# A scan and a feed-forward part joined into one program: quantisation beside the last scan group, last projection inside the first feed-forward step

## The reference

```python
# layer 0, first half
x_in = inp - mean(inp)
x, z = split(x_in @ W_in)                    # 256 + 256
x = silu(depthwise_conv4(x) + conv_b)
Bm, Cm = split(x @ W_x)                      # 16 + 16 states
delta = softplus(x @ W_dt + b_dt)
h[t] = exp(delta[t] * A) * h[t-1] + delta[t] * B[t] * x[t]   # for each of 256 x 16
y[t] = sum_s h[t, s] * C[t, s]
out = ((y + x * D) * silu(z)) @ W_out + inp
x = layernorm(x + out)
# layer 0, second half
xq, wq = fp4_quant_dequant(x), fp4_quant_dequant(w)   # blocks of 16: scale = max|.|/6, round to a grid
h = silu(xq @ wq_gate.T) * (xq @ wq_up.T)    # 352 hidden
x = layernorm(x + fp4_quant_dequant(h) @ wq_down.T)
# layer 1: attention, layernorm, three dense layers of signs, layernorm
```

## Time and profile before

| | |
|---|---|
| timed runs | 1086.28, 1090.7, 1086.28 us, median 1086.28 |
| the profiled execution | time 1083.86 us, span 1082.1 us |
| TensorE busy | 923.6 us (85%), 4482 matmuls; mean granted clock 0.959 |
| VectorE busy | 919.0 us (85%) |
| ScalarE busy | 726.4 us (67%) |
| GpSimd busy | 791.7 us (73%) |
| costliest groups | GpSimd drives 128 x 2359 ns; accumulations 512 x 622 ns; scans 184 x 1218 ns (into PSUM) and 72 x 1203 ns (into SBUF) |
| first VectorE instruction | 5.49 us |
| last scan product of VectorE | 470.83 us |
| first instruction of the third block | 483.54 us |
| first gate product | 488.02 us |

### The profile page before, as it was taken

How to read it: one execution, slowest core, us unless ns; L and a number is a source line. 1 busy time by engine, 2 the same in 40 slices (tenths; PEclk the granted TensorE clock), 3 DMA queues, 4 the chain that set the end, 5 groups by cost and what they waited for, 6 DMA issues and landing times. The chain is left out here.

```text
span 1082.1 us, 15503 instructions
## 1 busy us (share of the span) xinstructions
PE 923.6 (85%) x4482; PEld 482.3 (45%) x4482; DVE 919.0 (85%) x1446; ACT 726.4 (67%) x1536; POOL 791.7 (73%) x576
## 2 busy tenths in 40 slices
PE   6697989898979797756986779999999997799995
PEld 2233434343434342333654555555555543345454
DVE  4799999999999999967885477898989985689996
ACT  4776868686868686534565457777777767777872
POOL 2899999999998989945777734666676634877672
PEclk9899999998999999988899899999999999999998
DMA  4752515252535353006000222333333220000001
GB/s 149 311 235 78 236 78 229 85 211 102 197 116 197 117 197 117 1 23 122 1 0 11 87 80 85 95 90 90 91 87 97 84 60 3 1 1 11 19 20 30
DMA packets 35164, 103.97 MB, mean 96 GB/s; under 512 B 3659, under 2 KB 22475, under 8 KB 24395
## 3 DMA queue, kind: packets, MB, share of 16 engines
q1 hardware_dynamic: 35095, 103.16, 27.9%
HBM read 93.84 MB, written 8.91 MB: 95 GB/s over the span
## 5 line engine op out<-in xcount | busy, mean ns | idle before, releaser
L586 PE MATMUL m_yac<-m_hC,ident 128*128 128x512 f32 x512 | 255.7, 622 | 60.7 <-POOL m_hC L554 22.1
L544 POOL TENSOR_TENSOR m_dBu<-m_du,m_Bt 128x1024 f32<-128x1024 f32 x128 | 299.6, 2359 | 10.7 <-DMA m_Bt<-bcd 9.7
L331 DVE TENSOR_TENSOR_SCAN m_dA<-m_dA,m_dBu 128x512 f32<-128x512 f32 x184 | 222.2, 1218 | 17.1 <-ACT m_dA L456 13.3
L1302 DVE TENSOR_REDUCE a_nm<-bank 128x2 f32<-128x512 f32 x256 | 168.9, 683 | 43.0 <-PE bank L1533 41.0
L1472 ACT ACTIVATE late<-bank 128x512 f32<-128x512 f32 x256 | 150.5, 598 | 72.0 <-PE bank L1533 70.4
L586 PEld LDWEIGHTS m_yac<-m_hC,ident 128*128 128x128 f32 x512 | 93.3, 195 | 205.3 <-issue 111.3
L456 ACT ACTIVATE m_dA<-m_delta,early 128x510 f32<-128x510 f32 x256 | 169.9, 677 | 0.3
L340 DVE TENSOR_TENSOR m_hC<-m_dA,m_Ct 128x512 f32<-128x512 f32 x184 | 122.7, 667 | 0.0
L554 POOL TENSOR_TENSOR m_hC<-m_hS,m_Ct 128x512 f32<-128x512 f32 x72 | 94.7, 1315 | 24.8 <-DVE m_hS L331 24.8
L1533 PE MATMUL bank<-ks,qs 72*128 72x256 bf16 x512 | 98.8, 276 | 15.9 <-DMA ks<-parts 8.0
L453 ACT ACTIVATE m_dA<-m_zero 128x2 f32<-128x2 f32 x181 | 31.3, 173 | 114.0 <-DVE m_hC L340 113.5
(11 more groups left out here) (218 smaller groups left out, 1851.4 us busy)
## 6 DMA issues: line engine op xcount, KB each, us to landing
m_Bt<-bcd SPq DMA_DIRECT2D x32, 1024.0 KB, 6.1
m_Ct<-bcd SPq DMA_DIRECT2D x32, 1024.0 KB, 6.6
qs<-parts SPq DMA_DIRECT2D x16, 576.0 KB
ks<-parts SPq DMA_DIRECT2D x48, 192.0 KB
parts<-a_part SPq DMA_DIRECT2D x32, 192.0 KB, 2.2
out<-x_all SPq DMA_DIRECT2D x8, 256.0 KB, 2.3
vx<-in_vrow SPq DMA_DIRECT2D x4, 256.0 KB
qs<-in_fill SPq DMA_DIRECT2D x1, 768.0 KB
```

Of the source, the lines that this page charges most:

```text
L331: nc.vector.tensor_tensor_scan(out, decay, dBu[:, g % RD], 0.0, ALU.mult, ALU.add).then_inc(scan_ready, 1)
L544: nc.gpsimd.tensor_tensor(dBu[:, g % RD:g % RD + CH], du[:, n % 2], Bt[:, s].unsqueeze(1).broadcast_to([P, CH, GTOK]), ALU.mult).then_inc( ...
L586: return nc.tensor.matmul(out, lhsT, rhs, start=start, stop=stop)
L1302: nc.vector.tensor_reduce(nm[:, slot % 2, q, 2 * pair:2 * pair + 2], s1[i % 2][:], AX.X, ALU.max, negate=True).then_inc(max_ready, 1)
```

## The change

There is one block. SyncE's loads stand at the head of its part of it (`load`). The scan's functions now take a second argument `beside(i)`, called after each unit i of the last group, and return a `tail(n)`, which is interleaved piece by piece with the feed-forward steps n = -1, 0 and 1.

- `beside`: VectorE quantises x group 0 at units 4 (scales), 6 (abs, magic) and 15 (back), GpSimd its middle at 10; TensorE turns the weights at 1, 6 and 11 and x group 0 at 18, ScalarE copies at 8, 13, 18 and 25. They share bank 4. The scales of x group 0 lie in PSUM bank 5, not in SBUF, so the projection of group 6 (unit 16) waits for `qx.back`.
- `tail`: VectorE's `leave` of the last group in step -1, piece 2; `project_out` in step 0, piece 5, `squares` piece 6, `rstds` piece 7; `normalize` in step 1, piece 1.
- The product back of x group 1 is issued in step 0, piece 1, not at the end of step -1.
- PSUM: the scan uses banks named for the whole kernel, decays in 7, 0, 2, 1, sums in 6 and 3, the rest in 4 and 5. SBUF: the scan's tiles are given back and later parts' tiles lie over them; the turned weights lie where the weights were.
- SyncE's loads of constants wait for the last `normalize`.

The diff, cut to its core (indentation as after; the bodies of the scan's functions are the same):

```diff
-    with ctx:
...
-        dA = [ps(f"dA{i}", [P, 2, SEQ]) for i in range(RA)]
-        yac = [ps(f"yac{c}", [P, GTOK]) for c in range(CH)]
-        pp = [ps(f"pp{i}", [P, GTOK]) for i in range(2)]
+    ctx.close()
+    dA = [k.bank[i][:].rearrange("p (a b) -> p a b", a=2) for i in (7, 0, 2, 1)]
+    yac = [k.bank[i] for i in (6, 3)]
+    pp = k.bank[4:6]
...
+    def vector(dve, beside):
-            for n in range(GROUPS + 1):
+        for n in range(GROUPS):
...
-                        if n == GROUPS:
-                            quant_scale(nc, dve, k, k.qx, ffn_blocks(k, 0), 0)
-                            quant_abs(nc, dve, k.qx, 0)
-                            quant_magic(nc, dve, k.qx, 0)
...
+                if n + 1 == GROUPS:
+                    beside(i)
...
-            dve.wait_ge(norm_chain, GROUPS)
+        def tail(n):
+            for u in range(m.MARKS):
+                if n == -1 and u == 2:
+                    leave(GROUPS - 1)
+                yield
...
+                if n == 0 and u == 6:
+                    squares(GROUPS - 1)
+                if n == 1 and u == 1:
+                    normalize(GROUPS - 1)
...
+                if n == 0 and u == 7:
+                    rstds(GROUPS - 1)
...
+            if m == GROUPS - 2:
+                pe.wait_ge(k.qx.back, 1)
...
+                if n == 0 and u == 5:
+                    project_out(GROUPS - 1)
...
+    wts = k.wts[:]
+    wgT = wts[:, 0:HID]
...
+    def beside_vector(dve):
+        def at(i):
+            if i == 4:
+                dve.wait_ge(scan.z_took, 2 * GROUPS)
+                dve.wait_ge(scan.norm_chain, 1)
+                quant_scale(nc, dve, k, qx, ffn_blocks(k, 0), 0)
+            if i == 6:
+                quant_abs(nc, dve, qx, 0)
+                quant_magic(nc, dve, qx, 0)
+            if i == 15:
+                quant_back(nc, dve, qx, 0)
...
-        back_x(0)
...
+            if n == 0:
+                back_x(1)
...
-            if has(n + 2):
+            if has(n + 2) and n >= 0:
                 back_x(n + 2)
...
+    def beside_gpsimd(pool):
+        def at(i):
+            if i == 10:
+                quant_middle(nc, pool, qx, 0)
...
+    def beside_scalar(act):
+        def at(i):
+            if i in (8, 13):
+                n = (i - 8) // 5
+                act.wait_ge(w_turned, n + 1)
+                nc.scalar.activation((wgT, wuT)[n], th[0][:, 0:HID], ACT.Copy).then_inc(w_copied, 1)
...
+            if i == 25:
+                took_x(act, 0)
...
+    def beside_tensor(pe):
...
+            if i == 18:
+                pe.wait_ge(w_copied, 3)
+                turned_x(pe, 0)
...
+                if n == 0 and j == 1:
+                    pe.wait_ge(scan.y_step, 2 * GROUPS)
...
     def sync(sp):
+        sp.wait_ge(scan.norm_chain, GROUPS)
         sp.dma_start(k.identb[:], k.identb_dram).then_inc(k.identb_loaded, 16)
...
+            scan_end = scan_part(eng, beside_part(eng))
             ffn = ffn_part(eng)
-            for n in range(-1, f.LONE):
+            for n in range(-1, 2):
+                side_by_side(ffn(n), f.MARKS, scan_end(n), m.MARKS)
+            for n in range(2, f.LONE):
                 alone(ffn(n))
```

More of the change, by code:

```diff
@@ L703, in ffn_phase, with sb, sem, col @@
-def ffn_phase(nc, k):
+    def sb(name, shape, dt=F32):
+        return ctx.enter_context(nc.sbuf_tensor("m_" + name, shape, dt))
+    def sem(name):
+        return k.ctx.enter_context(nc.semaphore("m_" + name))
+    def col(name):
+        a, b = MAMBA_COLS[name]
+        return k.mprm[:, a:b]
+    w_in, w_x, w_dt, w_out = col("w_in"), col("w_x"), col("w_dt"), col("w_out")
+    conv_r, conv_b, b_dt, skip, decay = (col(x) for x in ("conv_r", "conv_b", "b_dt", "skip", "decay"))
+    ident = k.ident[:]
@@ L1010, in step, with turned_x @@
             yield
-            m = n + 1
-            if has(m):
-                act.wait_ge(x_turned, m + 1)
-                wait(act, up_ready, GT * (m - 1))
-                nc.scalar.activation(xqT[:, m % 2], th[0][:], ACT.Copy).then_inc(x_copied, 1)
+            if has(n + 1) and n >= 0:
+                took_x(act, n + 1)
             yield
         return step
+    def turned_x(pe, m):
+        pe.wait_ge(x_back, m + 1)
+        wait(pe, h_copied, min(GT * (m - 3) + 3, GT * GROUPS))
+        src = qx.out.rearrange("p (a b) e -> p a (b e)", a=GT)
+        for j in range(GT):
+            last = nc.tensor.transpose(th[0][:, P * j:P * j + P], src[:, j], k.ident[:])
+        last.then_inc(x_turned, 1)
@@ new lines, in beside_tensor, with at @@
+    def beside_tensor(pe):
+        ident = k.ident[:]
+        wq = qw.out.rearrange("p b e -> p (b e)")
+        def at(i):
+            if i == 1:
+                pe.wait_ge(qw.back, 1)
+                pe.wait_ge(scan.z_took, 2 * GROUPS - 1)
+            if i in (1, 6):
+                n = (i - 1) // 5
+                wait(pe, w_copied, n)
+                for c, (at, rows) in enumerate(HC):
+                    a = (len(HC) * n + c) * DM
+                    last = nc.tensor.transpose(th[0][:, at:at + rows], wq[0:rows, a:a + DM], ident[0:rows, 0:rows])
+                last.then_inc(w_turned, 1)
+            if i == 11:
+                pe.wait_ge(w_copied, 2)
+                for c, (at, rows) in enumerate(HC):
+                    a = 2 * len(HC) * DM + at
+                    last = nc.tensor.matmul(th[0][0:rows, P * c:P * c + P], wq[:, a:a + rows], k.center[:],
+                                            start=True, stop=True)
+                last.then_inc(w_turned, 1)
+            if i == 18:
+                pe.wait_ge(w_copied, 3)
+                turned_x(pe, 0)
+        return at
@@ L1020, in tensor @@
     def tensor(pe):
         ident = k.ident[:]
-        pe.wait_ge(qw.back, 1)
-        wq = qw.out.rearrange("p b e -> p (b e)")
-        for n, dst in enumerate((gp[0], up[0])):
-            for c, (at, rows) in enumerate(HC):
-                a = (len(HC) * n + c) * DM
-                last = nc.tensor.transpose(dst[:, at:at + rows], wq[0:rows, a:a + DM], ident[0:rows, 0:rows])
-            last.then_inc(w_turned, 1)
-        for c, (at, rows) in enumerate(HC):
-            a = 2 * len(HC) * DM + at
-            last = nc.tensor.matmul(th[1][0:rows, P * c:P * c + P], wq[:, a:a + rows], k.center[:],
-                                    start=True, stop=True)
@@ L1101, in step @@
             yield
-            turn_x(n + 1)
+            if has(n + 1) and n >= 0:
+                turned_x(pe, n + 1)
             down(n - 2, 3)
```

968 lines of the change are left out of this document (488 added, 480 removed).

## The result

| | before | after |
|---|---|---|
| median of the timed executions, us | 1088.49 (4: 1086.28 to 1092.75) | 1075.51 (4: 1073.02 to 1080.87) |
| profiled execution, time and span, us | 1083.86, 1082.1 | 1077.57, 1075.8 |
| its mean granted TensorE clock | 0.959 | 0.957 |

The ratio is 0.9899, with a 95% interval of 0.9868 to 0.9929: 11.0 us faster, between 7.7 and 14.4 (the two medians themselves lie 13.0 apart). The forecast was 1076.5 us and 9.8 us faster.

The account below looks back on a forecast made before the run. VectorE was taken to bound the last scan group, and chains of short links the start and seam. Gains of 1.3 and 8.5 (12.5 + 1.0 - 5.0) sum to 9.8 us: 1086.28 to 1076.5, range 1071 to 1082.

Parts of the forecast that it names:

- The start, +1.3: Kernel start: without waiting for the load block, the first convolution matmul comes at about 9.8 instead of 11.05, gaining 1.3 us.
- This time does not move: Start: the w_out product's weight load, released by the DMA of the parameters' last part, still begins at 8.41 us.
- The term's lower end, 0: Start: gain 0 if TensorE is at its lower clock level in the convolution's first matmuls.
- The last group, +5.0: Last scan group: VectorE pays 5.0 us net for eight added operations of the first x group (3.85 - 0.71 + 1.9).
- The wait of abs: Last scan group: abs waits 1.9 us for GpSimd's work under way, while magic finds GpSimd idle.
- The 0.71 for ScalarE's decay: Last scan group: VectorE's earlier 0.71 us scan wait for ScalarE's decay disappears, as scale operations now stand ahead of it.
- The seam, 13.5 saved (12.5 and 1.0): Between scan and feed-forward: 19.93 us shrinks to 7.45, saving 12.5; hidden tile 0 ahead of the product back saves 1.0.
- Its inputs are there: Seam: step 0's hidden tile 0 has its inputs, with the 1.28 us Silu table load beside leaving products and magic.
- What moved behind it: Steps 0 and 1: last projection, squares, power and normalising, a 7.6 us chain, stay hidden with 1.5 us to spare.
- 9.8 us earlier throughout: Attention part: unchanged in itself, so the whole 9.8 us gain persists there; anything else would show the forecast wrong.
- Rival B's first branch: Start gives nothing, one of three single-term failures that together put the time at 1077.8 to 1079.0 us; joint chance 0.15.
- Rivals A and D: Last group: no GpSimd wait, 1074.6 us, chance 0.12; scan: moved tiles slow each scan, 1092 at 60 ns, chance 0.05.

Follow-up runs that it names:

- the load block: Changed kernel with SyncE's loads again a block of their own in front of the program; first scan at 36.89 and 36.34 us in two traces.
- four products: Changed kernel plus four 512-column products on zeros in TensorE's pauses at the start; convolution 7.03 us, first scan at 33.57 us.
- the candidate: Changed kernel with abs and magic at unit 4, three products on zeros at the start, w_out product behind four convolution units; median 1070.69 us.
- its two variants: Three-edit kernel with Silu table loaded behind ScalarE's last group; then also x group 1's product back behind the second hidden tile; 1070.25 and 1073.43 us.

## Why the prediction was right, and where not

- **The start, +1.3: failed.** The convolution's first product came at 9.85 us where 9.8 was foretold, but that this is right to 0.05 is luck in part. The sentence on the transfer that the w_out product waits for, "This time does not move", was not true: the weight load behind it began at 8.83 instead of 8.41, and load and matmuls together took 1.02 us instead of 1.39. In the four other traces of this start the convolution began at 8.93 to 9.49. The failed sentence is the next one: "What follows up to the first scan hangs on these matmuls and moves with them." From the convolution's end to the first scan it is 15.5 to 16.2 us in all fourteen traces, so what follows does move with them. But they don't keep their length: 8.79 us instead of 7.14, because the clock rose at 13.4 us instead of 10.2. Why it rose late is open. TensorE starts earlier and pauses longer in this trace (1.42 us ahead of w_out), but the two traces with the load block had the kernel before's rows there and rose later still. The term's lower end, 0, named this case, and it is what came: the first scan is 0.44 us later than before. (Group 7 starts 0.13 us earlier all the same, because the fifth group of the kernel before took 55.71 us instead of 55.14, with a stretch at 0.50 from 249.2 us on.) With the pauses filled the convolution took 7.03 to 7.14 us in each of five traces (four products, the candidate twice, its two variants), at clock 1.00 from its first matmul.
- **The last group, +5.0: right, 4.66 paid.** The wait of abs was priced at 1.9 and cost 1.87; magic met GpSimd idle. The 0.71 for ScalarE's decay was absorbed, as there is no idle time ahead of a scan. The 0.3 less is probably what neighbouring instructions of VectorE overlap (about 0.1 each in the rows); no run tests it.
- **The seam, 13.5 saved (12.5 and 1.0): right, 13.6.** From last product to the end of back 7.45 was foretold and 7.37 came. Scale 2.20 for 2.25, leaving 1.20 for 1.29, magic to back 3.84 for 3.91. "Its inputs are there", said of hidden tile 0, was not so: it waited 1.36 us for ScalarE behind the table load. But it did so in GpSimd's time, which is why it cost nothing.
- **What moved behind it: right.** The projection ran at clock 1.00, step 1's hidden tiles don't wait for TensorE, and with the scan's end taken out of the steps the seam is 7.1 us longer.
- **The attention part, "9.8 us earlier throughout": wrong for a single pair of traces.** The distance was 10.5 us at 670, 9.5 from 750 to 855 and 6.3 at the end, through two stretches that were lost in this execution. The second trace of the changed kernel, against the same trace of the kernel before, is 9.4 to 9.7 us ahead from 750 us to the end.
- **The sum.** 9.8 foretold, 9.1 by the marks at hidden tile 1 (8.0 to 9.4 over the four pairs of two traces each), 11.0 (7.7 to 14.4) by the times. The number was right with one term of it empty, and that it came so near is luck in that much: the other two terms gave 8.96 us for 8.5, the start took 0.44, and 0.57 are what the kernel before lost in its fifth group. What separates 9.1 from 11.0 is smaller than what executions differ by. Rival B's first branch (the start gives nothing) is the mechanism that took place. Rivals A and D are out by rows: abs 2.30, scans 1213 and 1204 ns.

## What to carry to other kernels

When work at a kernel's start is moved earlier, ask what TensorE does in the pauses: a matmul that came while the clock was low took twice as long (0.85 for 0.43 us). The earlier start alone gained nothing against the kernel before, though 2.6 us against the same program with the load block; with two of the pauses filled and one product moved away, the first scan came 1.9 us earlier than the mean of five traces. An elementwise operation on VectorE that shares GpSimd's ports is to be put where the trace shows GpSimd waiting for VectorE, not merely where VectorE has a slot. And before a named wait is attacked, look at the next wait on the same engine: if that one has another releaser, it takes over in full.

## What was not expected of the hardware

- TensorE's granted clock fell to 0.50 in the middle of a busy stretch (856.5 us, for 6.8 us) in one execution and not in another of the same kernel, with the same short waits ahead of it (0.99 and 0.21 us in both), at a price of 2.7 us. The Trainium skill ("TensorE: Matmul & The Clock Gate", Part 1) says that the moments at which the gate decides aren't tied to the kernel's own start; the two traces agree, but no run here shows what it decides by.
- At the start the clock rose 4.6 to 11.0 us behind TensorE's first instruction where there were pauses (nine traces), and 3.4 to 5.5 where they were filled (five). The two ranges overlap, and where the pauses were filled TensorE also began earlier (2.59 us, 3.8 to 5.6 without), so no run tells which of the two helps. In the second trace of the changed kernel the clock rose only at 14.6 us, although TensorE had worked without a pause from 8.47 on.
- The second to seventh scan groups take 55.1 to 55.2 us, and 55.7 to 55.8 in nine cases: each of those had a stretch at 0.50 around its beginning that lasted 6.8 us instead of 3.4 (from 249.2 us in the kernel before, for one). The stretches of 3.4 cost nothing there.
